# Attention values on eight 64x32 array tiles, the convolution ahead of them, the high part first in the output projection, and other transfer layouts

## The reference, cut to what is computed

```
def _L0_cond_ref(...):   # h = gelu MLP of cond_128, att = softmax
    agg_w = jnp.einsum('bk,koi->boi', att, weight[..., 0])
    agg_b = att @ bias_k
    return jnp.einsum('boi,bih->boh', agg_w, x) + agg_b[:, :, None]
def _L0_attn_ref(x, Wq, Wk, Wv, Wo):
    q, k = _rope(q), _rope(k)
    scores = jnp.einsum('bkgqd,bkmd->bkgqm', qg, k) / np.sqrt(HEAD_DIM)
    attn = jax.nn.softmax(jnp.where(causal, scores, -jnp.inf), axis=-1)
    out = jnp.einsum('bkgqm,bkmd->bkgqd', attn, v)
    return out.reshape(b, s, HIDDEN) @ Wo
def _L0_cond2_ref(x, c, weight, c_weight, bias):
    out = lax.conv_general_dilated(x, weight, padding=[(4, 4)], feature_group_count=4, ...)
    return out + (c @ c_weight.T)[:, :, None] + bias[None, :, None]
def _L0_ffn_ref(...):
    base_out = x @ base_W.T + base_b
    # softmax of 15 router logits, top 8, mapped to 8 experts: w
    h = jnp.einsum('btd,erd->bter', x, A)
    return base_out + jnp.einsum('bter,eor->bto', h * w[..., None], B) * 2.0
x = x + _L0_attn_ref(_L0_cond_ref(x, cond_128, ...), Wq, Wk, Wv, Wo)
x = x + _L0_ffn_ref(_L0_cond2_ref(x, cond_128, ...), ...)
```

## Time and profile before

| | before |
|---|---|
| median of 3 runs | 660.11 us (657.11 to 661.21) |
| the profiled execution, its own time | 660.98 us |
| its span on the core | 659.1 us (1.9 us lie around it) |
| PE busy | 627.8 us, 95% |
| DVE, ACT, POOL busy | 72%, 30%, 34% |
| mean granted PE clock | 0.974 |
| PE on the chain that ended last | 88% |
| DMA | 71.2 MB, 108 GB/s |

### The profile page before, as it was taken

One profiled execution on the slowest core, in us unless ns is written; L12 is line 12 of the kernel. 1 busy time (PEld: TensorE's weight loads), 2 busy tenths in 40 slices (PEclk: granted clock), 3 DMA queues, 4 the chain that ended last, 5 costly groups with the idle time before them and its releaser, 6 DMA issues.

```text
span 659.1 us, 13009 instructions
## 1 busy us (share of the span) xinstructions
PE 627.8 (95%) x4375; PEld 512.9 (78%) x4375; DVE 476.9 (72%) x1169; ACT 200.2 (30%) x475; POOL 224.5 (34%) x181
## 2 busy tenths in 40 slices
PE   5967999999999999999999999999999999999785
PEld 3646888888888888888888888888888888887534
DVE  3555787777887777777788777777778777777612
ACT  4332333233333233323233323332323332332200
POOL 6341333323332333332333333333233333332200
PEclk9997999999999999999999999999999999999956
DMA  7675443544545544344444555434444455433410
GB/s 171 119 215 157 105 108 81 113 88 98 118 116 119 120 120 106 100 86 85 107 118 116 120 120 118 104 98 83 85 116 119 116 120 120 119 87 79 100 41 16
DMA packets 121300, 71.20 MB, mean 108 GB/s; under 512 B 48341, under 2 KB 103285, under 8 KB 121032
## 3 DMA queue, kind: packets, MB, share of 16 engines
q1 hardware_dynamic: 119808, 70.53, 45.7%
q10 hardware_dynamic: 1336, 0.24, 0.2%
q0 software_dynamic: 144, 0.28, 0.2%
HBM read 51.49 MB, written 19.53 MB: 108 GB/s over the span
## 4 chain that ended last, share of the span: by engine, by line
PE 88%; DVE 4%; DMA 4%; SPq 1%; ACT 1%; issue 1%; ACTq 0%; DVEq 0%
PE ps L389 32%; PE ps L559 9%; PE ps L553 8%; PE ps L612 6%; PE ps L571 5%; PE ps L579 5%; PE ps L489 4%; PE ps L525 4%; PE ps L600 4%; DMA mixw_dram<-scratch 2%; PE ps L587 2%; PE ps L543 2%; PE ps L433 2%; PE ps L567 2%; DMA xm<-x 1%; PE ps L526 1%
## 5 line engine op out<-in xcount | busy, mean ns | idle before, releaser
L869 POOL TENSOR_TENSOR qk<-network,t 128x640 f32<-128x640 f32 x31 | 48.2, 1555 | 171.1 <-DVE t L1046 171.1
L389 PE MATMUL ps<-wqkv_hi,y_hi 128*128 128x512 f32 (+1 forms) x256 | 87.5, 342 | 1.6 <-DVE raw L1065 1.5
L389 PE MATMUL ps<-wqkv_hi,y_lo 128*128 128x512 f32 (+1 forms) x256 | 87.3, 341 | 0.0
L389 PE MATMUL ps<-wqkv_lo,y_hi 128*128 128x512 f32 (+1 forms) x256 | 87.1, 340 | 0.0
L881 POOL TENSOR_TENSOR raw<-x1p,basebB 128x512 f32<-128x512 f32 x32 | 49.3, 1541 | 81.8 <-DVE x1p L1119 81.8
L1054 DVE TENSOR_TENSOR qk_t<-ps,cst 128x512 f32<-128x512 f32 x32 | 22.1, 692 | 58.5 <-PE ps L541 58.5
L694 ACT ACTIVATE qk_t<-ps 128x512 f32<-128x512 f32 x32 | 19.1, 597 | 141.5 <-PE ps L543 141.5
L694 ACT ACTIVATE raw<-ps 128x256 f32<-128x256 f32 (+1 forms) x96 | 40.2, 453 | 65.8 <-PE ps L600 64.1
L756 ACT ACTIVATE raw<-raw 128x512 f32<-128x512 f32 x64 | 40.4, 632 | 55.3 <-DVE raw L1065 55.3
L853 POOL TENSOR_TENSOR raw<-raw,rz 128x512 f32<-128x512 f32 x32 | 33.6, 1051 | 66.9 <-DVE rz L1075 66.9
L389 PEld LDWEIGHTS ps<-wqkv_hi,y_hi 128*128 128x128 f32 x256 | 48.7, 190 | 9.3 <-DVE raw L1065 1.9
(11 more groups left out here) (180 smaller groups left out, 1488.8 us busy)
## 6 DMA issues: line engine op xcount, KB each, us to landing
scratch<-x_dram SPq DMA_DIRECT2D x96, 256.0 KB, 5.0
x_dram<-x1p SPq DMA_DIRECT2D x32, 260.0 KB, 2.2
xm<-x SPq DMA_DIRECT2D x32, 256.0 KB, 3.5
xr<-x SPq DMA_DIRECT2D x32, 256.0 KB, 2.7
out<-raw SPq DMA_DIRECT2D x32, 256.0 KB, 2.1
v_dram<-vS SPq DMA_DIRECT2D x32, 64.0 KB
vB<-v_dram SPq DMA_DIRECT2D x128, 16.0 KB, 2.1
mixb<-mixb_dram SPq DMA_DIRECT2D x1, 1792.0 KB, 8.2
```

The lines of the kernel that those rows point to most:

```text
L389: last = mm(dst, a, b, start=(n == 0), stop=(n == 3 * len(left) - 1))
L869: nc.gpsimd.tensor_tensor(qk[:, :], t1, t2[:, :], ALU.add).then_inc(qk_sb, 1)
```

## The change

- **Values.** Each product of 128 rows x 64 columns becomes two of 64 rows x 32 columns. `vB` holds two heads side by side, the mask `kvmask` swaps the heads' pairs in odd sequences, and the results go to column strips and to banks 4 and 7 such that eight tiles of the array are used. 16 products in place of 8. The copies to `oT_hi` and `oT_lo` become two each (even and odd sequences). ACT's three copies of p out of PSUM become two. In the hardware loop a product of 2 columns without a use stands ahead of `values`.
- **Order.** `conv(t-1)` moves ahead of `values(t)`. `lora` does its 384-column terms first and then the 128-column ones, with a semaphore each. `project` does all products with `oT_hi` first and waits for `oT_lo` only before the last four.
- **Transfers.** `v_dram` is written in two DMAs, `vB` is read in eight. `x1_dram` is laid out by row, so that a partition's `xc` row is one run of 2078 elements; the write of x1 has runs of 130 elements.
- **Start and end.** `xm(2)` is issued before the base weights; the mixing weights and `mixb` for the later groups are loaded after `load_values(1)`. `keep_warm` uses 128-row `fp32r` products, 16 in all in place of 28, in the gaps of steps 32 and 33.

```diff
-        vB = sb("vB", [P, NB, 2, HK * HD])
+        vB = sb("vB", [P, 2, NB // 2, 2, 2 * HD])
...
-        v_dram = nc.dram_tensor("v_dram", [P, P], F32, kind="Internal").ap()
-        x1_dram = nc.dram_tensor("x1_dram", [NB * PH, CG * PH, P + 2], F32, kind="Internal").ap()
+        v_dram = nc.dram_tensor("v_dram", [S, 2, NB // 2, P], F32, kind="Internal").ap()
+        x1_dram = nc.dram_tensor("x1_dram", [CG * PH, NB * PH, P + 2], F32, kind="Internal").ap()
...
                 sp.wait_ge(vS_sb, u + 1)
-                sp.dma_start(v_dram.rearrange("(m b) c -> b m c", b=NB), vS[:, :]).then_inc(v_out, 16)
-                sp.wait_ge(v_out, 16 * (u + 1))
-                for k in range(HK):
+                for b in range(NB // 2):
+                    sp.dma_start(v_dram[:, :, b, :].rearrange("m a c -> a m c"), vS[2 * S * b:2 * S * (b + 1), :]).then_inc(v_out, 16)
+                sp.wait_ge(v_out, 16 * (NB // 2) * (u + 1))
+                for a in range(2):
+                    for k in range(HK):
...
             sp.dma_start(xr[:, :], group(x_g, 0)).then_inc(xr_in, 16)
+            sp.wait_ge(y_ps, 2)
+            sp.dma_start(xm[:, :], group(x_g, 2)).then_inc(xm_in, 16)
             sp.dma_start(rawbase, baseW.rearrange("(p j) l -> p j l", j=PH)).then_inc(ld["base"], 16)
...
                     for s in range(SHIFTS):
-                        sp.dma_start(xc[S * s:S * (s + 1), :, :],
-                                     x1_dram[:, :, s:s + P].rearrange("q r n -> r q n")).then_inc(xc_in, 16)
+                        sp.dma_start(xcF[S * s:S * (s + 1), 0:x1_row],
+                                     x1_dram.rearrange("r q n -> r (q n)")[:, s:s + x1_row]).then_inc(xc_in, 16)
                 if live(t + 1):
                     load_values(t + 1)
+                if peeled(t, 0):
+                    late_mixing()
...
-                    sp.dma_start(x1_dram.rearrange("q (i j) n -> (q i) j n", j=PH), x1p[:, :, :]).then_inc(x1_out, 16)
+                    sp.dma_start(x1_dram.rearrange("r q n -> q r n"), x1p[:, :, :]).then_inc(x1_out, 16)
...
-                    mm(ps[:, 0, :], query16[0:S, :], causal16[0:S, :], start=True, stop=True)
+                    mm(ps[:, 0, :], wo_hi[:, 0, 0:P], wo_hi[:, 1, :], start=True, stop=True)
...
+                pe.wait_ge(pT_sb, 2 * t + 2)
+                if not isinstance(t, int):
+                    mm(ps[0:S, 4, 0:2], convW[:, 0, :, :].rearrange("p j o -> p (j o)"), xc[:, 0, 0:2], start=True, stop=True)
                 for b in range(NB):
-                    if b != 2:
-                        pe.wait_ge(pT_sb, 3 * t + (1, 2, 2, 3)[b])
                     for h in range(2):
-                        last = mm(ps[P // 2 * h:P // 2 * (h + 1), 4, b * P:(b + 1) * P], vB[:, b, h, :], prT[:, 2 * b + h, :],
-                                  start=True, stop=True)
+                        for r in range(2):
+                            rows = slice(2 * S * r, 2 * S * (r + 1))
+                            to = S * (2 * h + (r + b) % 2)
+                            last = mm(ps[to:to + S, 4 + 3 * (b % 2), b // 2 * P:(b // 2 + 1) * P],
+                                      vB[rows, b % 2, b // 2, h, :], prT[rows, 2 * b + h, :], start=True, stop=True)
...
-                if peeled(t, G):
-                    lora(t - 2)
-                    keep_warm(28)
-                if live(t - 1):
+                if peeled(t, G) or peeled(t, G + 1):
+                    keep_warm(3)
+                if peeled(t, G):
+                    lora(t - 2)
+                if live(t - 1) and not peeled(t, G - 1):
                     conv(t - 1)
+                if peeled(t, G):
+                    keep_warm(3)
+                if live(t):
+                    values(t)
                 if peeled(t, 1):
+                    pe.wait_ge(oT_lo_sb, 2)
                     prepare_base((2, 3))
...
                     act.wait_ge(o_ps, t + 1)
-                    copy(oT_hi[:, :, :, :], ps[:, 4, :].rearrange("p (b g q) -> p g b q", b=NB, g=NQ)).then_inc(oT_hi_sb, 1)
+                    for a in range(2):
+                        last = copy(heads(oT_hi, a), heads_ps(a))
+                    last.then_inc(oT_hi_sb, 1)
```

More of the change, by code:

```diff
@@ L45 @@
 C_KV = C_CAUSAL + S
-C_SEQ = C_KV + HK
+C_SEQ = C_KV + NB * HK
 C_COS = C_SEQ + NB
@@ L59, in constants @@
     c[:, C_CAUSAL:C_KV] = np.where(m[None, :] <= (r % S)[:, None], 0, MASKED)
-    c[r, C_KV + r // HD % HK] = 1
+    for b in range(NB):
+        c[r, C_KV + HK * b + (r // HD + 2 * (b % 2)) % HK] = 1
     c[r, C_SEQ + r // S] = 1
@@ L345, in _, with late_mixing @@
             sp.dma_start(mixw_dram[4 * NB:B, :, :], aggS[4 * NB:B, :, :]).then_inc(mixw_out, 16)
-            sp.wait_ge(mixw_out, 16)
-            load_mixw(sp, 4, G, mixw_in)
-            sp.dma_start(mixb[:, 4 * P:], mixb_row[4 * P:].partition_broadcast(P)).then_inc(mixb_in2, 16)
+            def late_mixing():
+                sp.wait_ge(mixw_out, 16)
+                load_mixw(sp, 4, G, mixw_in)
+                sp.dma_start(mixb[:, 4 * P:], mixb_row[4 * P:].partition_broadcast(P)).then_inc(mixb_in2, 16)
             def steps(t):
-                if live(t + 2):
+                if live(t + 2) and not peeled(t, 0):
                     sp.wait_ge(y_ps, t + 2)
@@ L523, in lora @@
                 pe.wait_ge(hwT_lo_sb, u + 1)
-                for n, (a, b) in enumerate(((hwT_hi, lora_hi), (hwT_hi, lora_lo), (hwT_lo, lora_hi))):
-                    mm(ps[:, 6, 0:BASE6], a[:, :], b[:, 0:BASE6], start=False, stop=(n == 2))
+                terms = ((hwT_hi, lora_hi), (hwT_hi, lora_lo), (hwT_lo, lora_hi))
+                for n, (a, b) in enumerate(terms):
+                    last = mm(ps[:, 6, 0:BASE6], a[:, :], b[:, 0:BASE6], start=False, stop=(n == 2))
+                last.then_inc(ffn_ps, 1)
+                for n, (a, b) in enumerate(terms):
                     last = mm(ps[:, 2, 0:P], a[:, :], b[:, BASE6:D], start=(n == 0), stop=(n == 2))
-                last.then_inc(ffn_ps, 1)
+                last.then_inc(last_ps, 1)
             def project(u):
                 pe.wait_ge(oT_hi_sb, u + 1)
-                pe.wait_ge(oT_lo_sb, u + 1)
-                o = [tuple(w[:, g, :, :].rearrange("p b q -> p (b q)") for w in (oT_hi, oT_lo)) for g in range(NQ)]
-                product(ps[:, 3, :], o, [(wo_hi[:, g, :], wo_lo[:, g, :]) for g in range(NQ)]).then_inc(wo_ps, 1)
+                wait(pe, x1_sb, u)
+                for n, (a, b) in enumerate(((oT_hi, wo_hi), (oT_hi, wo_lo), (oT_lo, wo_hi))):
+                    if n == 2:
+                        pe.wait_ge(oT_lo_sb, u + 1)
+                    for g in range(NQ):
+                        last = mm(ps[:, 3, :], a[:, g, :, :].rearrange("p b q -> p (b q)"), b[:, g, :],
+                                  start=(n == 0 and g == 0), stop=(n == 2 and g == NQ - 1))
+                last.then_inc(wo_ps, 1)
             def transpose_qk(t):
@@ L795, in steps @@
                 if live(t):
-                    for n, (bank, lo, hi) in enumerate(((2, 0, 2), (3, 2, 6), (5, 6, 8))):
-                        act.wait_ge(pT_ps, 3 * t + 1 + n)
-                        copy(prT[:, lo:hi, :].rearrange("p k n -> p (k n)"), ps[:, bank, 0:(hi - lo) * P]).then_inc(pT_sb, 1)
+                    transposed_p(t, 0)
+                if live(t) and peeled(t, G - 1):
+                    transposed_p(t, 1)
                 if live(t - 2):
@@ L801, in steps @@
                     copy(hwT_hi[:, :], ps[:, 7, 0:P]).then_inc(hwT_hi_sb, 1)
+                if live(t) and not peeled(t, G - 1):
+                    transposed_p(t, 1)
                 if live(t):
                     act.wait_ge(o_ps, t + 1)
-                    copy(oT_hi[:, :, :, :], ps[:, 4, :].rearrange("p (b g q) -> p g b q", b=NB, g=NQ)).then_inc(oT_hi_sb, 1)
+                    for a in range(2):
+                        last = copy(heads(oT_hi, a), heads_ps(a))
+                    last.then_inc(oT_hi_sb, 1)
                 if live(t + 1):
@@ L1090, in low_oT @@
                 dve.wait_ge(oT_hi_sb, t + 1)
-                minus(oT_lo[:, :, :, :], ps[:, 4, :].rearrange("p (b g q) -> p g b q", b=NB, g=NQ),
-                      oT_hi[:, :, :, :]).then_inc(oT_lo_sb, 1)
+                for a in range(2):
+                    last = minus(heads(oT_lo, a), heads_ps(a), heads(oT_hi, a))
+                last.then_inc(oT_lo_sb, 1)
             def conv_bias(t):
```

50 lines of the change are left out of this document (34 added, 16 removed).

## The result

The changed kernel takes 733.21 us (median of 4 runs, 726.57 to 733.8) against 660.66 for the kernel before on the same chip: a ratio of 1.108, with a 95% interval of 1.101 to 1.116. I had forecast 680 us in a range of 636 to 697. The direction was right and the time lies outside the range. The profiled execution has a span of 732.0 us against 659.1.

What follows compares the result with a forecast made beforehand. The kernel before was held to be bound by PE in the loop, the changed one by SP's round trip of 19.3 us. 659.1 + 29.8 (loop) + 3.4 (start) - 13.1 (end) gave 679.2 us of span, forecast 680, range 636 to 697.

Steps and rivals of the forecast that it cites:

- PE's work: Loop step on PE: convolution and values fall from 2.23 to 1.74 us, so PE alone would need 17.86 us.
- The rival of two row tiles taking turns on one bank: Values on PE: halves sharing a PSUM bank take turns, values about 1.2 us, round trip 19.9, 697 us; chance 0.07.
- The round trip: SP's chain from one step's convolution through v, vB, x1 and xc to the next convolution: 19.3 us, bounding the step.
- the open terms: SP's round trip: vB issues at 0.45 (-1.2 us) or xc landing in 4.3 (-1.0) make the kernel faster, 638 us; chance 0.30.
- The write of x1: SP's round trip, from x1's write to the release of the xc loads: 2.3 us, up to 2.6 for shorter runs.
- The eight reads: SP's round trip, eight vB reads: 0.6 us to issue each, 4.8 us in all, bounds 2.7 and 5.2.
- `xc` at 5.75 for 5.3: SP's round trip, xc loads up to the convolution: 5.3 us, in the middle between 4.3 and 6.3.
- The world that I had forecast: Loop: round trip 19.3 us exceeds PE's 17.86, so conv(t-1) waits about 1.4 us every step; chance 0.50.
- the port rule: xc loads: 32 partitions reach only half the DMA ports; by it about 5.9 us, without it 4.3.
- The start: Up to conv(1): xm(2) in time, but conv(0) waits some 10 us, conv(1) at 88.7: +3.4 us, bounds 0 and 6.
- The end: Last steps: fewer fillers and some clock back, projection about 1 us later: -13.1 us, bounds -10 and -16.
- The clock, rival of 0.03: Loop: gaps in every step lower the granted clock, some steps at half clock, time above 700 us; chance 0.03.

Runs made afterwards that it cites:

- e8_all: Changed kernel with the old x1 layout, x1's write between the vB reads, xr and xm behind xc, late mixing weights behind the first xc: 632.5 us.
- e3b_behind: Changed kernel with the convolution behind the values again, slow write of x1 kept: 675.3 us, ratio 1.023 to the kernel before.
- e1_x1_rows: Changed kernel with x1_dram and the xc loads laid out as before (write in 128 rows of 2080 bytes): 666.4 us, ratio 1.010 to the kernel before.
- e4_late: Changed kernel with the late mixing weights and mixb loaded behind the first xc loads in step 1: 725.7 us.
- e11_end: Kernel before with 4 in place of 28 filling matmuls in front of the last convolution: 649.4 us, ratio 0.985.
- e12_fill: Changed kernel with eight filling matmuls of 512 columns in front of each convolution of the loop: 729.4 us.
- e6_loads: Changed kernel with xr and xm loaded behind xc on SP, not right behind the write of x1: 721.4 us.
- e2_pitch: Changed kernel with rows of x1p and x1_dram of 144 values in place of 130, the number of runs the same: 725.4 us.

## Why the prediction was right or wrong

**PE's work, right.** I had 17.86 us for PE alone; e8_all measures 17.83 a step at the mean and 17.86 at the median. The values took 0.60 us (343.87 to 344.47) where I took 0.65, and the product of 2 columns 0.13 where I took 0.1. The rival of two row tiles taking turns on one bank falls: 32 passes of 128 columns, two row tiles to a bank, in 0.60 us; four tiles at a time would have taken 1.0 by the 0.125 us for a pass that I took from the convolution, an estimate. The rule of the Trainium skill that I weighed there (TensorEngine Tiling (Array Packing), "Gotcha 1: PSUM Pressure") does not show as lost time in this trace.

**The mechanism, right.** The round trip became the bound, with the convolution's wait in each step released by `xc`, and the new order was its cause (e3b_behind) together with the write (e1_x1_rows). My ranking holds too: the `vB` issues and `xc` were the open terms. But I treated as settled the term that was the largest miss.

**The write of x1, the step that failed: 2.3 predicted, 4.5 measured.** I wrote "write of x1 2.3 (2.18, and shorter runs, up to 2.6)". The old row was for 128 rows of 2080 bytes; the change makes 512 runs of 520 bytes of it, and I gave that 0.4 us at most. It landed 4.5 us after its issue at the median, 4.8 in the step shown, and 2.4 with the old rows put back (e1_x1_rows). Its bound should have been taken from a row with as many short runs, such as `xc` with 512 runs a load landing in 3.7 to 5.4 us. Had I kept 5.4 as the upper bound, the range would have reached to a step of 19.3 + 3.1 = 22.4 us.

**The eight reads, mis-sized the other way: 4.8 predicted, 3.65 measured.** Halving the runs did shorten an issue, from 0.607 to 0.432 us at the median; eight in a row take 3.65, 0.456 each. With `xc` at 5.75 for 5.3, the mean step's sum is off by +2.2 for the write, -1.3 for the reads and what follows them, and +0.45 for `xc`: +1.4. Over 29 steps the loop's mean of 20.69 for 19.3 is 40 us of the 53 missed. The world that I had forecast exists: in e1_x1_rows, with the write at 2.4 and the reads at 3.64, my sum becomes 18.2, and the step is 18.56. So the conclusion that I drew from the earlier trace rows, that the number of runs is not what an issue costs, was wrong for these reads, though the 896 runs in 0.544 us stand: an issue's cost goes by more than one thing. By luck this error hid more than half of the other.

**The weighing of the port rule.** I had said that `xc` by the skill's half of the ports (SBUF — State Buffer, "Door 1: The DMA port swizzle") would be near 5.9 and without it 4.3. The measured 5.7, with nearly the same in e1 (5.9) where the runs are 512 bytes, shows that the long runs gave only 0.1 us. That agrees with the 5.9 and speaks against 4.3. But no run changed the partitions, and I treated three loads in flight together as one load of 32 partitions, so the rule itself is not shown.

**The start: +3.4 predicted, +9.6 measured.** conv(0) came at 71.35, not 67, after 15.5 us rather than 10: `mixb` was issued at 55.87, since I had left out the 2.2 us in which four loads of `mixw` are issued, and x1(0)'s write landed 1.8 us behind it rather than with it. Then conv(0) to conv(1) took 23.5 rather than 21.5 us, since behind the long wait PE runs at half clock for over 8 us (granted clock 0.50 from 71.35 to 80.00, the convolution 1.93 us); e8_all, with 1.00 there, takes 21.0. The 10.2 us at 0.50 that I quoted for the kernel before include 4.8 us of the wait for `xm`; PE was busy for 5.39 of them. The place and the cause were as I put them, as e4_late shows.

**The end: -13.1 predicted, -6.8 measured.** The 28 matmuls were worth what I said (e11_end: 43.8 to 30.6, 13.2 us). But in step 31 the round trip bounds too, and PE is ready for the convolution sooner, since no queries of a next group lie in between (16.09 us from convolution to convolution before, against 18.35 in the loop): the convolution there waits 5.07 us, then PE runs at half clock (0.52 from 694.99 to 705.00). I counted 1 us for that.

**The clock, rival of 0.03.** I gave it over 700 us. The dips were there and cost some 4 us (e12_fill). The time above 700 had another cause.

## What to carry to other kernels

When a change puts more on a chain of transfers, every transfer whose shape it changes needs its own bound, from a row with as many runs of that length, above all the one that seems small; here that was the write of x1. Read what stands between two transfers on the issuing queue: moving the write sooner alone gave 34 us, moving the loads out of its way alone 12, and both 83. And before a chain is shortened by putting work elsewhere, ask what the work was covering: the convolution in front of the values hides 0.9 us of waiting for copies, and costs nothing once the round trip fits.

## What the runs showed of the hardware

- The landing of 260 KB from SBUF to DRAM, at the median: 2.4 us in 128 rows of 2080 bytes (e1_x1_rows), 4.5 in 512 runs of 520 bytes, 4.1 with the 520-byte runs but two loads of 256 KB issued behind the next loads and not right behind it (e6_loads). 288 KB in 512 runs of 576 bytes: 3.5 (e2_pitch).
- An issue on SP takes 0.432 us at the median for 128 runs of 64 bytes and 0.607 for 256 of them; a write of x1 takes 0.34 to 0.37 us in long rows and 0.58 in short ones.
- Eight tiles of 64x32 run together: 32 passes of 128 columns of float32 in 0.60 us, with two row tiles writing one bank on different partitions.
- The granted clock of the loop was 0.95 with waits of 0.9 to 3.0 us in front of its convolutions (the changed kernel), and 1.00 with waits of 0.2 to 1.4 us (e1_x1_rows) and of 0.4 to 1.4 us (e12_fill).
